# Turning two weights by DMA transposes instead of TensorE products in a fused two-layer graph kernel

## The reference

```python
# layer 0: a graph over the 512 nodes, shared by all items
x_norm = xn / max(norm(xn), 1e-12);  mean_sim = einsum('nbl,mbl->nm', x_norm, x_norm) / B
A = mean_sim kept at each row's k = 153 largest entries other than its own
deg = A.sum(0);  dinv = rsqrt(deg);  An = dinv[:, None] * A * dinv[None, :]
x = layernorm(x + einsum('sd,sbl->dbl', An, einsum('nbl,lo->nbo', xn, adj)) + bias)
# layer 1: h = x, per item a causal graph over its 128 rows
z_l = h @ W_lang.T;  z_g = h @ W_grav.T;  v = h @ W_V.T
A_l = relu(cosine(z_l, z_l)),  A_g = exp(-dist2(z_g, z_g) / 2 sigma^2),  no diagonal, causal, rows made to sum to 1
out = (w * K_l + (1 - w) * K_g) @ v @ W_O.T
x = layernorm(x + out)
```

## Time and profile before

| | |
|---|---|
| median of 3 runs | 914.11 us (913.64 to 914.65) |
| the profiled execution | 914.44 us, of it span 912.7 us, 1.7 us around the span |
| PE busy | 893.0 us (98%) |
| DVE, ACT, POOL busy | 756.7 (83%), 576.3 (63%), 239.1 us (26%) |
| granted TensorE clock, mean | 0.995 |
| chain that ended last | PE 89%, DVE 6%, DMA 2%, ACT 1%, issue 1% |

### The profile page before, as it was taken

One profiled execution on the slowest core, in us unless ns is written; L12 is line 12 of the kernel. 1 busy time (PEld: TensorE's weight loads), 2 busy tenths in 40 slices (PEclk: granted clock), 3 DMA queues, 4 the chain that ended last, 5 costly groups with the idle time before them and its releaser, 6 DMA issues.

```text
span 912.7 us, 18592 instructions
## 1 busy us (share of the span) xinstructions
PE 893.0 (98%) x6706; PEld 535.5 (59%) x6706; DVE 756.7 (83%) x1743; ACT 576.3 (63%) x1067; POOL 239.1 (26%) x246
## 2 busy tenths in 40 slices
PE   8999999999999999999999999999999999999995
PEld 6777887565556565656565656555555555555452
DVE  5888588868888888888888888888888888888867
ACT  6887567795757565656666666666666656562523
POOL 3888354042212121222222222222222222220100
PEclk9999999999999999999999999999999999999998
DMA  7552320201433332323233323233333323241211
GB/s 302 189 204 102 130 93 6 87 3 36 82 81 83 80 86 75 95 71 100 64 98 67 106 57 111 55 108 56 105 60 101 63 98 68 94 65 52 59 47 47
DMA packets 105114, 79.56 MB, mean 87 GB/s; under 512 B 81904, under 2 KB 82032, under 8 KB 103152
## 3 DMA queue, kind: packets, MB, share of 16 engines
q1 hardware_dynamic: 105072, 79.02, 31.3%
HBM read 42.80 MB, written 16.81 MB: 65 GB/s over the span
## 4 chain that ended last, share of the span: by engine, by line
PE 89%; DVE 6%; DMA 2%; ACT 1%; issue 1%; POOL 0%; SPq 0%; DVEq 0%
PE bank L261 16%; PE bank L263 16%; PE bank L262 16%; PE pair L261 8%; PE pair L263 8%; PE pair L262 8%; PE bank L517 2%; PE bank L523 2%; PE bank L524 2%; PE pair L517 1%; PE bank L487 1%; DMA arena<-arena 1%; DMA arena<-in_x 1%; PE pair L502 1%; PE bank L502 1%
## 5 line engine op out<-in xcount | busy, mean ns | idle before, releaser
L261 PE MATMUL bank<-arena 128*128 128x512 f16 (+2 forms) x1056 | 290.4, 300 | 3.4 <-DMA arena<-arena 1.7
L262 PE MATMUL bank<-arena 128*128 128x512 f16 (+2 forms) x1056 | 291.2, 300 | 0.0
L263 PE MATMUL bank<-arena 128*128 128x512 f16 (+2 forms) x1056 | 291.1, 300 | 0.0
L438 POOL TENSOR_TENSOR arena<-arena 128x512 f16<-128x512 f32 x59 | 68.4, 1159 | 358.6 <-ACT arena L1199 314.4
L261 PE MATMUL pair<-arena 128*128 128x512 f16 (+1 forms) x400 | 150.4, 376 | 0.0
L262 PE MATMUL pair<-arena 128*128 128x512 f16 (+1 forms) x400 | 150.4, 376 | 0.0
L263 PE MATMUL pair<-arena 128*128 128x512 f16 (+1 forms) x400 | 150.3, 376 | 0.0
L261 PEld LDWEIGHTS bank<-arena 128*128 128x128 f16 x1056 | 103.3, 98 | 64.5 <-DMA arena<-arena 3.2
L263 PEld LDWEIGHTS bank<-arena 128*128 128x128 f16 x1056 | 103.3, 98 | 62.9
L262 PEld LDWEIGHTS bank<-arena 128*128 128x128 f16 x1056 | 103.3, 98 | 58.6 <-issue 0.7
L448 POOL TENSOR_TENSOR arena<-arena 128x512 f16<-128x512 f32 x56 | 64.9, 1161 | 166.0 <-ACT arena L1069 166.0
(11 more groups left out here) (368 smaller groups left out, 1884.4 us busy)
## 6 DMA issues: line engine op xcount, KB each, us to landing
arena<-in_x SPq DMA_DIRECT2D x32, 1024.0 KB, 5.5
out_dram<-arena SPq DMA_DIRECT2D x15, 1024.0 KB, 4.3
arena<-rn_dram SPq DMA_DIRECT2D x15, 256.0 KB, 3.9
arena<-arena SPq DMA_TRANSPOSE x74, 3.2
arena<-in_x SPq DMA_DIRECT2D x2, 512.0 KB, 4.6
arena<-in_w_grav_t SPq DMA_DIRECT2D x1, 1024.0 KB, 7.6
arena<-in_w_lang_t SPq DMA_DIRECT2D x1, 1024.0 KB, 5.3
arena<-in_w_v SPq DMA_DIRECT2D x1, 1024.0 KB, 8.1
```

Of the source, the lines that this page charges most:

```text
L261: pe.matmul(dst, ah, bh, start=start, stop=False)
L262: pe.matmul(dst, ah, bl, start=False, stop=False)
L263: return pe.matmul(dst, al, bh, start=False, stop=stop)
L438: pool.tensor_tensor(h_l[:, b, :], h[slot][:, b, :], h_h[:, b, :], ALU.subtract).then_inc(s["hl_ready"], 1)
```

## The change

W_lang and W_grav get their scale and their high and low parts in the layout in which they came, and the parts are turned afterwards, high and low together, by eight DMA transposes from SP's queue (128x1024 float16 each, the form in which h is turned in the bodies). `turn_weight`, `less_high`, `turned_high`, `turned_low`, `ident_w` and `ident_neg` go. ACT gets `weight_scaled` and `weight_part`, POOL gets `weight_low`: eight pieces of 128x256 for each weight. Of W_lang's upper products three move ahead of `mix_nodes`; `needs_along(1)` moves behind W_grav's first. dinv goes to bank 7.

```diff
+        wn = [at(k * KIB, [2 * KB, NODES], F16) for k in (48, 56)]
+        w_parts = [at(k * KIB, [KB, 2 * NODES], F16) for k in (64, 72)]
-        ident_w = [at(196 * KIB + KIB // 2 + i * KIB // 2, [P]) for i in range(2)]
-        ident_neg = at(197 * KIB + KIB // 2, [P], F16)
@@ sync
             sp.dma_start(xg[0], x_group[0]).then_inc(s["x_in0"], 16)
+            for n, i in enumerate((1, 0)):
+                for k in range(KB):
+                    sp.wait_ge(s["w_low_made"], n * KB + (k + 1))
+                    sp.dma_start_transpose(wn[i][:, :, k * P:(k + 1) * P], w_parts[i][:, k, :]).then_inc(s[f"wn_in{i}"], 16)
@@ gpsimd: behind adj_l
+            def weight_low(n, i):
+                pool.wait_ge(s["w_high_made"], n + 1)
+                half = NODES // 2
+                for k in range(KB):
+                    for c in range(0, NODES, half):
+                        last = pool.tensor_tensor(w_parts[i][:, k, NODES + c:NODES + c + half],
+                                                  w_raw[i][:, k, c:c + half], w_parts[i][:, k, c:c + half], ALU.subtract)
+                    last.then_inc(s["w_low_made"], 1)
+            weight_low(0, 1)
             pool.wait_ge(s["x_h_ready"], GB)
             low(blocks(first_x_l), blocks(first_x), blocks(first_x_h), 8, s["x_l_ready"])
+            weight_low(1, 0)
@@ tensor
             def upper_product(i, d):
-                pe.wait_ge(s["wn_out"], (2 - i) * KB)
+                pe.wait_ge(s[f"wn_in{i}"], KB * 16)
...
-            vo_product(0)
-            less_high(1, 0)
-            less_high(1, 1)
+            vo_product(0, range(0, 1))
+            pe.wait_ge(s["S_ready"], 6)
+            turn(bank[7][:, P:2 * P], 2, 3).then_inc(s["S_turned"], 1)
+            vo_product(0, range(1, KB))
             vo_product(1)
-            turn_weight(1, 2)
-            turn_weight(1, 3)
             vo_product(2)
             degrees(range(0, 2))
-            less_high(1, 2)
-            less_high(1, 3)
             vo_product(3)
-            needs_along(1)
             for b in range(GB):
                 first_project(b)
-            for d in range(KB):
+            upper_product(1, 0)
+            needs_along(1)
+            for d in range(1, KB):
                 upper_product(1, d)
+            upper_product(0, 0)
             degrees(range(2, KB))
-            turn_weight(0, 0)
-            turn_weight(0, 1)
+            upper_product(0, 1)
...
-            less_high(0, 0)
-            less_high(0, 1)
-            turn_weight(0, 2)
-            turn_weight(0, 3)
+            upper_product(0, 2)
...
-            less_high(0, 2)
-            less_high(0, 3)
...
-            upper_product(0, 0)
             first_turn(0)
             first_turn(1)
-            upper_product(0, 1)
+            upper_product(0, 3)
             first_turn(2)
             first_turn(3)
-            upper_product(0, 2)
-            upper_product(0, 3)
@@ scalar: behind adj_h
+            def weight_scaled(i):
+                act.activation(w_raw[i], w_raw[i], ACT.Copy, scale=up[:, i:i + 1]).then_inc(s["wn_scaled"], 1)
+            def weight_part(n, i):
+                act.wait_ge(s["wn_scaled"], n + 1)
+                act.activation(w_parts[i][:, :, 0:NODES], w_raw[i], ACT.Copy).then_inc(s["w_high_made"], 1)
+            weight_scaled(1)
+            weight_part(0, 1)
+            weight_scaled(0)
@@ scalar: behind the Gram stage
-            turned_low(1, 1)
-            deviation(1)
             act.wait_ge(s["w_scaled"], 3)
             act.wait_ge(s["w_l_ready"], 2)
             act.activation(first_x_h, first_x, ACT.Copy).then_inc(s["x_h_ready"], GB)
+            deviation(1)
+            weight_part(1, 0)
+            for d in range(KB):
+                vo_out(d)
@@ vector: in scales
-                for i in range(2):
-                    dve.tensor_scalar(ident_w[i], ident[:], up[:, i:i + 1], None, ALU.mult).then_inc(s["scale_ready"], 1)
```

More of the change, by code:

```diff
@@ L375, in _ @@
             pool.memset(magn[:], 1.0).then_inc(cs, 1)
-            pool.memset(ident_neg, 0.0).then_inc(cs, 1)
             pool.memset(eps_c[:], LN_EPS).then_inc(cs, 1)
-            pool.wait_ge(cs, 8)
+            pool.wait_ge(cs, 7)
             pool.affine_select(out=ident[:], in_=ident[:], compare_op=ALU.not_equal, fill=1.0, base=0,
@@ L393, in _ @@
                                base=0, pattern=[[-1, P]], channel_multiplier=1).then_inc(s["picks_made"], 1)
-            pool.affine_select(out=ident_neg, in_=ident_neg, compare_op=ALU.not_equal, fill=-1.0, base=0,
-                               pattern=[[-1, P]], channel_multiplier=1).then_inc(s["picks_made"], 1)
             for c in range(NC):
@@ L623, in project_x @@
                 mm.then_inc(s["xw_ps"], 1)
-            def turn_weight(i, j, ks=range(KB)):
-                n = (1 - i) * KB + j
-                pe.wait_ge(s[f"w_in{i}"], 16)
-                pe.wait_ge(s["scale_ready"], 4)
-                wait(pe, s["wn_out"], n - 1)
-                for k in ks:
-                    mm = pe.matmul(bank[4 + j % 2][:, k * P:(k + 1) * P], w_raw[i][:, k, j * P:(j + 1) * P],
-                                   ident_w[i], start=(k == 0), stop=(k == KB - 1), skip_group_check=True)
-                if ks[-1] == KB - 1:
-                    mm.then_inc(s["wn_ps"], 1)
             finish_diagonal(2)
             finish_diagonal(3)
-            turn_weight(1, 0, range(0, 2))
-            pe.wait_ge(s["S_ready"], 6)
-            turn(bank[7][:, P:2 * P], 2, 3).then_inc(s["S_turned"], 1)
-            turn_weight(1, 0, range(2, KB))
-            turn_weight(1, 1)
             def first_project(b):
@@ L653, in _, with vo_product @@
             OUT_OF_ROW = [2, 4, 6, 7]
-            def vo_product(d):
+            def vo_product(d, fs=range(KB)):
                 pe.wait_ge(s["w_l_ready"], 2)
@@ L658, in vo_product @@
                     pe.wait_ge(s["S_ready"], 8)
-                for f in range(KB):
+                for f in fs:
                     mm = three(pe, bank[d][:], vo_h[0][:, f, d * P:(d + 1) * P], vo_l[0][:, f, d * P:(d + 1) * P],
                                vo_h[1][:, f, :], vo_l[1][:, f, :], start=(f == 0), stop=(f == KB - 1))
-                mm.then_inc(s["vo_ps"], 1)
-            def less_high(i, j):
-                pe.wait_ge(s["wn_h_ready"], (1 - i) * KB + j + 1)
-                pe.matmul(bank[4 + j % 2][:], ident_neg, wn_h[i][:, j, :], start=False, stop=True,
-                          skip_group_check=True).then_inc(s["wn_rest"], 1)
+                if fs[-1] == KB - 1:
+                    mm.then_inc(s["vo_ps"], 1)
             u_bank = [[bank[4 + d] for d in range(KB)], [bank[d] for d in range(KB)]]
             def upper_product(i, d):
-                pe.wait_ge(s["wn_out"], (2 - i) * KB)
+                pe.wait_ge(s[f"wn_in{i}"], KB * 16)
                 if i:
@@ L1089, in log_exp @@
                 act.activation(t[:, 2, :], t[:, 1, :], ACT.Exp, scale=-0.5).then_inc(done, 1)
-            def turned_high(i, j):
-                act.wait_ge(s["wn_ps"], (1 - i) * KB + j + 1)
-                act.activation(wn_h[i][:, j, :], bank[4 + j % 2][:], ACT.Copy).then_inc(s["wn_h_ready"], 1)
-            def turned_low(i, j):
-                act.wait_ge(s["wn_rest"], (1 - i) * KB + j + 1)
-                act.activation(wn_l[i][:, j, :], bank[4 + j % 2][:], ACT.Copy).then_inc(s["wn_out"], 1)
             def upper_out(i, d):
@@ L1173, in an_high @@
                 act.activation(an_h[:, i, :], A[:, i, :], ACT.Copy).then_inc(s["an_h_ready"], 1)
-            an_high(0)
-            an_high(1)
-            turned_high(0, 2)
-            an_high(2)
-            turned_high(0, 3)
-            an_high(3)
+            for i in range(KB):
+                an_high(i)
+            upper_out(0, 2)
             act.preload_act_table_set("natural_log_exp_and_others")
@@ L1353, in _ @@
             act.activation(vo_scale[:, 0:1], vo_scale[:, 1:2], ACT.Exp, scale=0.5).then_inc(s["vo_root"], 1)
-            for d in range(KB):
-                upper_out(0, d)
+            upper_out(0, KB - 1)
             upper_high(0)
@@ L1667, in _ @@
             dve.wait_ge(s["dinv_ps"], 1)
-            dve.tensor_reduce(c1(D_MAX), bank[6][:], AX.X, ALU.max).then_inc(ds_, 1)
+            dve.tensor_reduce(c1(D_MAX), bank[7][:], AX.X, ALU.max).then_inc(ds_, 1)
             dve.wait_ge(ds_, 7)
@@ L1681, in _ @@
             for i in range(KB):
-                dve.scalar_tensor_tensor(A[:, i, :], A[:, i, :], dinv_col[:, i:i + 1], bank[6][:], ALU.mult,
+                dve.scalar_tensor_tensor(A[:, i, :], A[:, i, :], dinv_col[:, i:i + 1], bank[7][:], ALU.mult,
                                          ALU.mult).then_inc(s["an_f"], 1)
```

32 lines of the change are left out of this document (8 added, 24 removed).

## The result

The changed kernel took 920.53 us (median of 4 runs, 918.38 to 922.26), the kernel before 914.38 us beside it (913.64 to 915.66): a ratio of 1.0068, with a 95% interval of 1.0049 to 1.0086. It is 6.15 us slower, where 5.8 was forecast, and 919.9 us lies 0.6 us from the median. The profiled execution was the fastest of the four: 918.38 us, span 916.6, mean granted clock 0.991.

A forecast was written before the change was run, and what follows sets the result against it. body(0)'s start sets the end, held by PE's queue and DVE's chain through A to mix_nodes, nearly side by side. -1.5 + 4.6 + 2.7 = +5.8 us on 914.1 gives 919.9 us, range 913.5 to 924.0.

The forecast's parts named there:

- What POOL's pieces cost DVE: On DVE's chain to A and mix_nodes: steps wait for POOL's new pieces, +4.6 us, bounds 0 and about 6.5.
- item 1: Last max correction, two keep passes and two self marks (130.6 to 134 us) each wait for a POOL piece: +1.9 us.
- item 2: Four dependent small DVE steps (L1489 to L1498) under first_x_l: +1.7 us, and one more at L1500: +0.4.
- item 3: Count rounds (L1508 to L1517) have eight POOL pieces beside them before and after: 0.
- item 4: DVE's L1538 to L1546, now under POOL's xw_l: +1.7 us.
- item 5: Late rounds (L1590 to L1598) get rid of POOL's pieces at 150.17 to 155.3 us, three waits less: -1.1 us.
- The clock: PE's idle stretches bring half clock: +1.7 us in front of body(0), +1.0 at 164 us, together +2.7.
- What is won behind `mix_nodes`: With upper products moved away, the layer norm decides and body(0) can start earlier after mix_nodes: -1.5 us, not -6.
- no collision: Rival: POOL's pieces and DVE's steps interleave, mix_nodes starts when it does now: 912.6 to 914.3 us, chance 0.12.
- the clock holds: Rival: DVE waits for POOL, but some products break PE's idle stretches and no clock loss comes: 917.2 us, chance 0.22.
- PE's queue held everything: Rival: DVE's chain stood behind PE, so mix_nodes starts before 163 us: 906.8 us, chance 0.08.
- late transposes: Rival: weights' DMA transposes land 3 us behind need, W_grav's products and needs_along(1) hold DVE: +2 us more, 922, chance 0.06.

The follow-up runs named there:

- dummy pieces: Kernel before plus 16 POOL pieces of weight_low's shape whose results nobody reads, eight behind adj_l and eight behind first_x_l: 920.45 us beside 914.82, ratio 1.0065.
- the gates: Changed kernel with POOL's pieces held back by constant waits on DVE's pick_steps, same work and output: 916.27 us beside 915.08, ratio 1.0012.
- one-column run: Changed kernel with POOL's 16 weight_low pieces subtracting one column each instead of 256, low parts left out: 918.39 us beside 914.82, ratio 1.0034.
- warm products: Changed kernel with 33 float32 products of ones and ident put into PE's waits, same output: 917.81 us beside 914.82, ratio 1.0031.
- old-places run: Changed kernel with W_lang's four upper products and ACT's evictions of them back behind mix_nodes: 921.3 us beside 915.08, ratio 1.0062.
- one-column gated run: Changed kernel with POOL held by waits on pick_steps, PE's idle time filled with products, weight_low's pieces cut to one column: 911.67 us beside 914.23, ratio 0.9974.

## Why the prediction was right

**What POOL's pieces cost DVE** (+4.6). By the durations of the steps themselves, before and after: item 1 (L1598, L1610, L1643) +0.17, +0.70 and +0.96, 1.8 where 1.9 was forecast; item 2 +1.63 and L1500 +0.19, where 1.7 and 0.4 stood; item 3 +0.2 for 0; item 4 3.71 instead of 1.82 us, +1.9 for 1.7; item 5 0.71 instead of 1.97, -1.3 for -1.1. That sums to 4.5, and the second `keep` is 4.97 us late. The other 0.5 us came before item 1, in `pick(0)`: L1590 (now L1560) took 1.32 us instead of 0.82 beside pieces of W_V and W_O, which stand there in both kernels, so no term had it. The dummy pieces show the cause, the gates its remedy. The comparison within one profile, the same line with and without a piece beside it, was what carried this.

The sentence on the Trainium skill (SBUF — State Buffer, "Who interferes with whom"), that `tensor_scalar` can be shut out too, proved right in the one-column run: L1454, two elements on a strided input, took 0.68 us where it met a piece, instead of 0.17. In the changed kernel it took 0.17 us although POOL was at work, so the 0.4 us more of the sum of 5.0 did not come, by luck of the moment. The same section says that with two inputs in SBUF `tensor_tensor` contends with POOL's reads and that the form with an accumulator doesn't take the shared pair; the traces agree, with 0.16 against 0.58 us for the one and 0.74 to 0.75 us either way for the counts.

**The clock** (+2.7). Half clock came twice while PE had work, at 162.0 and 185.9 us. DVE's wait for dinv's transposes rose from 0.75 to 2.12 us, +1.4 where 1.0 stood; in `body(0)` DVE's first pass over `gg` (L1803, L1836 before, over PE's products of one item with itself) came 20.35 us after the start of `body(0)` instead of 18.52, +1.8 where 1.7 stood. The warm products give 2.7 to 3.2 us back. The profile understates it a little. Its mean clock of 0.991 makes (1 - 0.991) x 2 x 916.6 = 16.5 us at half clock; 3.4 and 6.8 are the stretches above, and 6.5 lie behind 909 us, where PE has nothing more to do (5.0 in the kernel before). The run of 922.26 us had 0.987, which makes 24 us; where those 7 us lay isn't seen. A stretch of 3.4 us near the start, which the kernel before's profile has and this one lacks, would be one part. The Trainium skill (TensorE: Matmul & The Clock Gate, "What's actually happening") takes the low clock as the default and activity as what releases it. That fits the old-places run, in which PE, with sparse work, stayed at 0.50 for 17 us. The sum of 5.1 us drawn from it in the prediction, a cold stretch behind each pause, didn't come: in the changed kernel itself, and in the gated one, PE stood still for 2.84 us before the dense `mix_nodes` and the clock stayed at 1.00. In the kernel with the dummy pieces a pause of the same 2.84 us, ahead of the one-column degrees, was followed by half clock. What decides between the two was not tested.

**What is won behind `mix_nodes`** (-1.5). 18.5 us instead of 19.6 in the changed kernel, -1.1; 18.0 and so -1.6 with the clock held. The argument was right; part of its gain went into ACT and PE pauses of 1.3 and 1.5 us.

**What is hidden.** In the changed kernel W_grav's and W_lang's DMA transposes were never waited for; ACT's three activations fitted in, with 0.56 us of idle time left; `first_project` spread over 141.7 to 146.2 us, with the 1.6 us of the start 143.3 to 147.8, where 143 to 147 was forecast. All 0.

**What was not in the sum.** The 0.5 us of L1590, and h's transposes ahead of `body(1)`. PE's wait of 1.4 us for them was taken as unchanged, and it went. A transpose of h took at most 3.3 us to land instead of 4.5 there. With these, 4.97 + 0.1 (degrees) + 1.4 - 1.1 + 1.8 - 1.4 = 5.8 us for two executions that start alike. The profiled spans differ by 3.9, with the 1.58 us of the start by 5.5; the medians differ by 6.15.

So part of the nearness of 919.9 to 920.53 is luck. The collision came out 0.5 us dearer than forecast (with the 0.1 for the degrees), the clock 0.5, and 0.4 us less were won behind `mix_nodes`; against these 1.4 us stands the same amount for h's transposes, which the prediction had not foreseen. How much of that gain lasts isn't clear either: SP's DMA of `nl` (L343, L337 before), once for each group, stands 4.95 us later than in the kernel before in the first group, 4.06 in the second and 4.7 again in the third. Why the transposes land earlier stays open: kernels with the old weight path waited 1.2 to 1.4 us there in all three traces, those with the new one none or, in the warm run, 0.7, and no run was made to tell why.

The rivals: *no collision* fell with L1459 to L1468; *the clock holds* with two rows of PEclk at 0.50; *PE's queue held everything* with `mix_nodes` at 170.5 us, and with the one-column gated run, where the queue is short and `mix_nodes` still waits 0.60 us for DVE; *late transposes* with the list of waits.

## What to carry to other kernels

Before work is taken from the busiest engine and given to an idle one, look at what the receiver shares with a third. Here GpSimd stood idle for half of the stage, but a piece that it runs holds up VectorE steps with two SBUF operands and small `tensor_scalar` steps, and a chain of tiny dependent steps pays a whole piece per step. Find a line that runs with and without such a neighbour in the same profile and price it from there, and if the work must move, hold it with waits on the other engine's own progress so that it lands beside reductions, counts and max passes. Here that brought 1.0068 down to 1.0012, and no further.

TensorE's pauses aren't free even where nothing waits for them: behind a pause of 3.5 us and sparse work the clock was at half (though not behind one of 2.84 us and dense work). Put movable products into the pause, not behind it.

## What the runs showed of the hardware

- A VectorE `tensor_tensor` of 16 elements was held 5.26 us by a row of sixteen GpSimd subtractions of 128 columns (0.42 us each, 0.39 apart). In the changed kernel, with 256 columns (0.63 apart), no step was held for more than one piece's length. The long hold was seen once in one trace; why the shorter pieces left no gap stays open.
- VectorE steps of two elements take 0.16 us alone, and 0.3, 0.6 and 1.05 us beside GpSimd pieces of 128, 256 and 512 columns. Counts with an accumulator (0.75 us) did not change, nor did the `max` passes (0.69 us), `match_replace` (0.68 us) and `bn_stats` (two in 1.28 us).
- A granted clock of 0.50 came in stretches of 3.4, 6.8, 13.7 and 17.0 us. It lasted longest, 17.0 us, where PE was idle for 6.08 us and then had one-column products. 33 small float32 products in the changed kernel's pauses kept the clock at 1.00 from 120 to 260 us.
- A pause of PE of 2.84 us left the clock at 1.00 where dense products followed (changed, gated and one-column kernels, at `mix_nodes`) and was followed by 0.51 for 3.4 us where one-column products followed (kernel with dummy pieces, at the degrees).
- In executions of the kernel before at mean clocks of 0.996 and 0.997 the time was 912.2 to 913.1 us, beside a median of 914.23 for all twenty; one profile with a stretch of 3.4 us at half clock near the start is 1.6 us behind one without it.
